# A gated delta-rule layer on one core: decay factors made ahead and read back by DMA, an earlier seed transpose, another order of PSUM banks

## The chip, the cores and the metric

One core of one Trainium2 chip runs the whole program. The metric is device time in microseconds (us), from several runs of the same kernel. One execution is profiled, and all rows below come from it.

## The reference

The input is 8 sequences of 1024 tokens, 128 features each. A layer of gated delta-rule attention (8 heads of 128, 3 Householder steps per token) is followed by a mixture of 8 experts; both have a residual and a layer norm. Cut to what matters here:

```
beta = 2 * sigmoid(x @ Wb)                        # per token, step, head
g    = -exp(A_log) * softplus(x @ Wa + dt_bias)   # per token, head
def step(S, inp):
    qt, kt, vt, bt, gt = inp
    S = S * exp(gt)
    for i in range(3):
        S = S + bt_i * outer(kt_i, vt_i - kt_i @ S)
    return S, qt @ S
```

The kernel works on chunks of 32 tokens. Inside a chunk it needs, for each pair of tokens j and t, the decay `exp(sum of g over the tokens after j, up to t)`: a table of 32 x 32 numbers per chunk and head.

## The kernel before, in words

The program has three parts: a prologue (to about 165 us of the profile) that makes per-token tables for all 256 chunks; the attention loop; and the expert part, which the change doesn't touch.

**The loop** goes over 64 superchunks of 128 tokens, four chunks (c = 0 to 3) each. Two superchunks are one turn of the hardware loop, an even one and then an odd one, so the loop's jump stands between an odd superchunk and the next even one. Each chunk has 14 slots (k = 0 to 13), written out by hand on every engine. All is float32.

- **The projection.** Slot k of chunk c projects tile m = 14c + k of the superchunk's 56 tiles on TensorE (PE) into one of three PSUM banks of `PP` (`project`, L471, matmul L478). ScalarE (ACT) makes the first convolution tap (L692), VectorE (DVE) the other three one slot later (`tap`, L780, three instructions per slot: in its slot k it works on tile k - 1), ACT the SiLU (L769). The bank of tile m is m % 3. Since 56 isn't a multiple of 3, tiles 0 and 1 meet a bank used two tiles before and not three, and `project` waits for the taps of the tile two before instead of the one three before (L476).
- **The chunk's pipeline.** Preparation of one chunk (rows of K, Gram matrices, the decayed matrices U and UQ), inversion of a triangular matrix for the one prepared before (`invert`, eight stages in the slots of `INV_AT`, L493 and L495 on PE, `inv_out` L787 and L792 on DVE), and the run of an older one (`old_state` L507, joining L610 to L624, `solve`, `read_out` L544, `new_state` L552; on DVE BZ L834 and the state S L801).
- **The seed.** GpSimd (POOL) makes the seed Y1 (L986, L988). DVE transposes it into XB in slot 13, between taps (L884, instruction L795). PE's first inversion stage in slot 1 of the next chunk (L493) multiplies by XB.
- **The decay factors.** POOL makes, for each chunk, the table GM = g times a mask (`decay`, L940). In slot 0 of chunk 0, for the four chunks of a superchunk, PE multiplies GM by the mask `after` in two matmuls of 512 columns, into PB and PK (L593, L597), and ACT takes the exponential of both into EX (L697, L699). `rows_k` and the joining matmuls of slot 2 wait for ACT there (`e_sb`). POOL multiplies EX by per-row factors into E2 (L971), from which EM comes.
- **Extras.** Chunk 2 also carries the output of an older superchunk (FA L842, WO matmuls L668); chunk 3 has the gate (L663), QSE (L825), the transposed next input in slot 12 (L469, L918).

The order of instructions on each engine is the order of the code; PE, ACT, DVE and POOL each go through their slots in turn and wait on semaphores.

Of the kernel before, what the change touches and what calls it, by code (L numbers as in the profile page):

```python
# [10 lines left out]
P = 128  # L11
# [20 lines left out]


STAGES = ["W0", "H", "H1", "H2", "W1", "H", "H1", "H2"]
assert len(STAGES) == STEPS

# [77 lines left out]
def attention_part(nc, x, Wq, Wk, Wv, Wb, Wa, A_log, dt_bias, conv_q, conv_k, conv_v, Wg, rms_weight, Wo,  # L114
                   consts, x1):
    ctx = ExitStack()
    with ctx:
# [11 lines left out]

        xf = x.rearrange("b t d -> (b t) d")  # L130


# [32 lines left out]
        with pctx:  # L165
            def psb(name, shape):
# [9 lines left out]
            Z = psb("Z", [P, NCH, NHEAD])  # L176
            Z2 = psb("Z2", [P, NCH, NHEAD])
            PXT = pctx.enter_context(nc.psum_tensor("PXT", [P, 2, 512], F32))
# [3 lines left out]
            xl_in = sems("xl_in", 2)  # L182
            xlt_ps, xlt_sb, raw_ps, raw_sb, aw_sb, bt_sb = (sem(n) for n in (
                "xlt_ps", "xlt_sb", "raw_ps", "raw_sb", "aw_sb", "bt_sb"))
# [4 lines left out]
            with nc.Block() as block:  # L189
                @block.sync  # L190
                def _(sp):
# [19 lines left out]
                    with sp.Fori(1, NLOAD // 2) as t:  # L211
                        for b in range(2):

                            sp.wait_ge(xlt_ps, 2 * t + b - 1)
                            sp.dma_start(XL[:, b], xf[bass.ds((2 * t + b) * 512, 512)].rearrange("(q p) d -> p q d", p=P)).then_inc(xl_in[b], 16)

                @block.gpsimd
                def _(pool):
                    pool.memset(WALL[:, :, :], 0.0).then_inc(wz, 1)
                    pool.memset(ones[:, :], 1.0).then_inc(wz, 1)  # L220
                    pool.memset(half4[:, :], 0.5).then_inc(wz, 1)
                    pool.memset(mhalf[:, :], -0.5).then_inc(wz, 1)

                @block.tensor
                def _(pe):
# [22 lines left out]
                    for k in range(3 * NPC, 4 * NPC):  # L248
                        pe.wait_ge(tab_sb, k - 1)
                        piece = flat(BETA)[:, PIECE * (k - 3 * NPC):PIECE * (k - 3 * NPC) + PIECE]  # L250
                        pe.matmul(PTB[:, k % 2, 0:PIECE], perm, piece, start=True, stop=True).then_inc(tab_ps, 1)

                @block.scalar
                def _(act):
# [16 lines left out]
                    for k in range(3 * NPC, 4 * NPC):  # L271
                        act.wait_ge(tab_ps, k + 1)
                        act.activation(flat(BETA)[:, PIECE * (k - 3 * NPC):PIECE * (k - 3 * NPC) + PIECE], PTB[:, k % 2, 0:PIECE], ACT.Copy).then_inc(tab_sb, 1)

                @block.vector
                def _(dve):
# [24 lines left out]
                    for s, c in enumerate((13, 11, 9, 7, 5, 3)):  # L301
# [37 lines left out]
        KDS = sb("KDS", [P, NHEAD])  # L339
        GM = sb("GM", [P, CPS, NHEAD, CT])  # L340
        EX = sb("EX", [R, CPS, NHEAD, CT])
        E2 = sb("E2", [R, NHEAD, CT])
# [38 lines left out]
        quad = PB[:, :].rearrange("p (h c) -> p h c", h=4)  # L381
        ptile = lambda m: PP[:, m % 3, 0:HALO + P]
        row_bank = lambda l, h: (PA, PK)[l][0:R, h % LH]
        lanes = [slice(0, 4), slice(4, 8)]
        heads = [range(0, 4), range(4, 8)]

        ready, begun = sem("ready"), sem("begun")
# [4 lines left out]
        gm_sb, d_ps, e_sb, kr_ps, ssr_sb, sse_sb, r2_sb, rt_sb, s1_sb, kds_sb, e2_sb, em_sb, kd_sb, kk_ps, u_sb = (  # L392
            sem(n) for n in ("gm_sb", "d_ps", "e_sb", "kr_ps", "ssr_sb", "sse_sb", "r2_sb", "rt_sb", "s1_sb", "kds_sb",
                             "e2_sb", "em_sb", "kd_sb", "kk_ps", "u_sb"))
# [42 lines left out]
        with nc.Block() as block:  # L437
            @block.sync
            def _(sp):
# [25 lines left out]
            def _(pe):  # L465
# [44 lines left out]
                def rows_k(l, i, c, sc, prep, run):  # L510
                    pe.wait_ge(kqv_sb, TILES * i - (LH if l == 0 and c == 0 else 0))
                    if l == 0 and c == 0:
                        pe.wait_ge(e_sb, 2 * i)
                    need(pe, u_sb, 2 * prep - 1 + l)
# [62 lines left out]
                def program(i, half, c):  # L577
# [7 lines left out]
                    for k in range(SLOTS):  # L585
                        if do_inv and k in INV_AT:
                            invert(invn, 1 - par, INV_AT[k])
                        if known(i, 0, NSC):
                            project(i, half, SLOTS * c + k)
                        if k == 0 and c == 0 and do_prep:  # L590
                            side_bank_free(i, c, run, do_run)
                            pe.wait_ge(gm_sb, prep + CPS)
                            pe.matmul(PB[0:R, :], after, GM[R:P, 0:2], start=True, stop=True).then_inc(d_ps, 1)  # L593
                            need(pe, s_sb, 2 * run - 1)
                            need(pe, u_sb, 2 * prep - 1)
                            need(pe, vp_sb, 2 * prep)
                            pe.matmul(PK[0:R, 0:LH], after, GM[R:P, 2:4], start=True, stop=True).then_inc(d_ps, 1)  # L597
                        if k in (1, 4) and do_run:
# [3 lines left out]
                        if k == 2 and do_run:  # L602
                            pe.wait_ge(x3t_sb, run + 1)
                            if do_prep and c == 0:
                                pe.wait_ge(e_sb, 2 * i)
# [42 lines left out]
                        if k in (8, 10) and gate_now:  # L648
                            l = (k - 8) // 2
                            if l == 0:  # L650
                                if do_run:
                                    pe.wait_ge(join_sb, 3 * run + 3)
                                else:
                                    need(pe, e_sb, 2 * i)
                                if known(i - 2, 0, NSC):
# [24 lines left out]
            def _(act):  # L680
                def program(i, half, c):
# [4 lines left out]
                    for k in range(SLOTS):  # L686
                        if known(i, 0, NSC):
# [4 lines left out]
                            act.activation(CY[:, m % RING], ptile(m)[:, 0:P], ACT.Copy, scale=taps_of(m)[:, 0:1]).then_inc(tap0_sb, 1)  # L692
                        if k == 0 and c == 0 and do_prep:
                            need(act, e2_sb, 2 * prep)
                            flat = lambda t: t.rearrange("p c h t -> p (c h t)")
                            act.wait_ge(d_ps, 2 * i - 1)
                            act.activation(flat(EX[:, 0:2]), PB[0:R, :], ACT.Exp).then_inc(e_sb, 1)  # L697
                            act.wait_ge(d_ps, 2 * i)
                            act.activation(flat(EX[:, 2:4]), PK[0:R, 0:LH].rearrange("p h c -> p (h c)"), ACT.Exp).then_inc(e_sb, 1)  # L699
                        if k in (1, 3) and do_prep:  # L700
# [74 lines left out]
            def _(dve):  # L775
# [29 lines left out]
                def group(i, half, c, k, part):  # L805
# [133 lines left out]
            def _(pool):  # L939
                def decay(ahead, i, c):  # L940
                    need(pool, d_ps, 2 * i)
                    pool.tensor_tensor(GM[R:P, c], over(G[R:P, ahead, :], [CT, NHEAD, CT], 2),
                                       over(upto[:, R:P], [CT, NHEAD, CT], 1), ALU.mult).then_inc(gm_sb, 1)
                    pool.wait_ge(gm_sb, ahead + 1)

                def program(i, half, c):
                    ahead, prep, invn, run, do_ahead, do_prep, do_inv, do_run = when(i, c)
                    par = c % 2
                    if do_run:
                        pool.wait_ge(inv_sb, STEPS * (run + 1))  # L950
                        need(pool, z_ps, 2 * run)
                        for b in range(NBK):
                            r = slice(BK * b, BK * b + BK)
                            pool.tensor_tensor(YF[r, :, r], Y3[r, :, :], over(ones[r, 0:BK], [BK, NHEAD, BK], 1), ALU.mult).then_inc(diag_sb, 1)  # L954
                            pool.wait_ge(diag_sb, NBK * run + b + 1)
                    if do_ahead:
                        decay(ahead, i, c)
                    if c == 2 and known(i - 2, 0, NSC):
# [3 lines left out]
                    if do_prep:  # L962
                        for l in range(2):
# [7 lines left out]
                            pool.tensor_tensor(E2[:, hs], EX[:, c, hs], over(S1[0:R, hs], [R, LH, CT], 2), ALU.mult).then_inc(e2_sb, 1)  # L971
                            pool.wait_ge(e2_sb, 2 * prep + l + 1)
# [449 lines left out]
```

## Time and profile before

| | us |
|---|---|
| median of 3 runs (8914.47 to 8927.09) | 8919.44 |
| profiled execution, its own time | 8925.8 |
| its span, first to last instruction | 8924.0 |
| PE busy | 7944.6 (89%) |
| DVE busy | 6744.4 (76%) |
| ACT busy | 5415.4 (61%) |
| POOL busy | 3168.8 (36%) |

The granted TensorE clock has a mean of 0.913 of the full one. A busy figure is the time in which the engine had an instruction at work; where an engine waits, a row names what ended the wait. "issue" as a releaser means that the profile shows nothing waited for; at the loop's jump it is the time until an engine has its next instructions. In a stretch's row, the column "PEclk" is the clock that was granted to TensorE.

### The profile page before, as it was taken

How to read it: one execution, taken by the hardware profiler on the slowest of the kernel's cores; microseconds unless marked ns; L12 is line 12 of the kernel's file. 1: busy time of each engine (PE TensorE's matmuls, PEld its weight loads, DVE VectorE, ACT ScalarE, POOL GpSimd, SP SyncE). 2: the span in 40 equal slices, each digit the busy share in tenths (PEclk: the TensorE clock that was granted, in tenths of full speed). 3: DMA queues.
4: the chain of work that ended last, by engine and by line, in shares of the span. 5: the costliest groups of instructions: out<-in, count | busy, mean ns of one | idle time of the engine just before them, and what ended most of it. 6: DMA issues, size and time to landing. Idle time of an engine off the chain costs nothing. (4 is left out here: it accounts for less than half of the span.)

```text
span 8924.0 us, 423618 instructions
## 1 busy us (share of the span) xinstructions
PE 7944.6 (89%) x156132; PEld 6671.9 (75%) x156132; DVE 6744.4 (76%) x22809; ACT 5415.4 (61%) x19287; POOL 3168.8 (36%) x5052
## 2 busy tenths in 40 slices
PE   3888989898889888989889898989898988979999
PEld 2677777777777777777777777777777777767777
DVE  5888888888888888888888888888888888733333
ACT  2666666666666666666666666666666666623333
POOL 0333334443433334443334343443334434411111
PEclk6899999999999999999999999999999999889999
DMA  1000000000000000000000000000000000010000
GB/s 44 4 5 6 6 6 6 6 5 6 5 6 6 6 6 6 6 5 6 6 6 6 6 5 6 5 6 6 6 6 6 6 6 5 5 28 8 9 10 8
DMA packets 72477, 64.75 MB, mean 7 GB/s; under 512 B 16944, under 2 KB 67392, under 8 KB 69952
## 3 DMA queue, kind: packets, MB, share of 16 engines
q1 hardware_dynamic: 70208, 35.32, 1.4%
q8 instruction: 1323, 21.68, 1.1%
q14 instruction: 946, 7.75, 0.3%
HBM read 26.92 MB, written 8.39 MB: 4 GB/s over the span
## 5 line engine op out<-in xcount | busy, mean ns | idle before, releaser
L780 DVE SCALAR_TENSOR_TENSOR CY<-PP,CWV,CY 128x128 f32<-128x128 f32 x4608 | 1587.9, 345 | 109.0 <-DVE CY L780 6.3
L780 DVE SCALAR_TENSOR_TENSOR CY<-PP,CWK,CY 128x128 f32<-128x128 f32 x4608 | 1585.5, 344 | 77.0
L986 POOL TENSOR_TENSOR Y<-U,C 32x256 f32<-32x256 f32 x768 | 554.5, 722 | 1223.9 <-DVE UQ L861 1183.8
L478 PE MATMUL PP<-XT,WV 128*128 128x131 f32 x3072 | 781.7, 343 | 221.6 <-issue 118.3
L692 ACT ACTIVATE CY<-PP,CWK 128x128 f32<-128x128 f32 x1536 | 562.9, 366 | 543.0 <-PE PP L478 535.0
L954 POOL TENSOR_TENSOR YF<-Y,ones 32x256 f32<-32x256 f32 x768 | 551.5, 718 | 784.0 <-DVE Y L792 743.9
L495 PE MATMUL PI<-T,WB 32*32 32x32 f32 x49152 | 722.8, 192 | 120.1 <-DVE T L792 118.9
L478 PE MATMUL PP<-XT,WK 128*128 128x131 f32 x3072 | 768.8, 338 | 68.2 <-DVE CY L780 68.2
L705 ACT ACTIVATE EM<-PK 128x128 f32<-128x128 f32 x2048 | 538.6, 280 | 474.5 <-PE PK L519 474.4
L495 PEld LDWEIGHTS PI<-T,WB 32*32 32x32 f32 x49152 | 610.5, 107 | 272.2 <-issue 202.4
L692 ACT ACTIVATE CY<-PP,CWV 128x128 f32<-128x128 f32 x1536 | 560.1, 365 | 395.5 <-PE PP L478 388.4
L493 PEld LDWEIGHTS PI<-XB,U 32*32 32x32 f32 x24576 | 353.2, 118 | 534.6 <-issue 497.7
L769 ACT ACTIVATE KQ<-CY 128x128 f32<-128x128 f32 x2048 | 740.4, 362 | 8.3
L478 PEld LDWEIGHTS PP<-XT,WV 128*128 128x128 f32 x3072 | 503.6, 208 | 315.6 <-issue 129.7
L493 PE MATMUL PI<-XB,U 32*32 32x32 f32 x24576 | 407.9, 204 | 367.8 <-DVE XB L795 367.8
L1197 ACT ACTIVATE HS<-PH,B1S 128x512 f32<-128x512 f32 x512 | 352.7, 689 | 610.0 <-PE PH L1116 610.0
L801 DVE SCALAR_TENSOR_TENSOR S<-S,WHOLE,PK 128x128 f32<-128x128 f32 x2048 | 613.4, 342 | 141.5 <-PE PK L552 141.4
L507 PE MATMUL PA<-S,KQ 128*128 128x128 f32 x4096 | 702.2, 328 | 0.0
L1125 PEld LDWEIGHTS PY<-W2S,HS 128*128 128x128 f32 x4096 | 533.9, 192 | 217.9 <-issue 214.8
L834 DVE SCALAR_TENSOR_TENSOR BZ<-PA,HEADD,VP 128x128 f32<-128x128 f32 x2048 | 618.2, 345 | 82.3 <-PE PA L507 52.8
L507 PEld LDWEIGHTS PA<-S,KQ 128*128 128x128 f32 x4096 | 656.9, 243 | 0.7 <-issue 0.2
L966 POOL TENSOR_TENSOR S<-R,BETA 96x4 f32<-96x4 f32 x512 | 101.9, 199 | 1519.3 <-DVE R L821 1519.3
(231 smaller groups left out, 19750.7 us busy)
## 6 DMA issues: line engine op xcount, KB each, us to landing
XR<-in_L_attn_x SPq DMA_DIRECT2D x65, 64.0 KB, 1.9
XL<-in_L_attn_x SPq DMA_DIRECT2D x16, 256.0 KB, 2.8
XRES<-in_L_attn_x SPq DMA_DIRECT2D x64, 64.0 KB, 1.9
x<-X SPq DMA_DIRECT2D x64, 64.0 KB, 2.0
XI<-x SPq DMA_DIRECT2D x16, 256.0 KB, 3.1
out<-OUT SPq DMA_DIRECT2D x16, 256.0 KB, 2.3
W1S<-in_L_ffn_W SPq DMA_DIRECT2D x1, 2048.0 KB
WK<-in_L_attn_Wk SPq DMA_DIRECT2D x1, 1536.0 KB, 10.2
```

The lines of the kernel that those rows point to most:

```text
L478: pe.matmul(ptile(m), w, XT[:, half], start=True, stop=True).then_inc(proj_ps, 1)
L493: mm = pe.matmul(inv[r, h], U[r, par, h, r], XB[r, h], start=True, stop=True)
L495: mm = pe.matmul(inv[r, h], WB[r, h], term[r, h], start=True, stop=True)
L507: mm = pe.matmul(PA[:, h % LH], KQ[:, rs, h, rc], S[:, h], start=True, stop=True)
L692: act.activation(CY[:, m % RING], ptile(m)[:, 0:P], ACT.Copy, scale=taps_of(m)[:, 0:1]).then_inc(tap0_sb, 1)
L705: op = act.activation(EM[:, h], PK[:, h], ACT.Square, accum_out=SSR[:, c, h:h + 1])
L769: act.activation(to, CY[:, m % RING].rearrange("p (c t) -> p c t", c=CPS), ACT.Silu).then_inc(kqv_sb, 1)
L780: dve.scalar_tensor_tensor(CY[:, m % RING], ptile(m)[:, s:s + P], taps_of(m)[:, s:s + 1], CY[:, m % RING], ALU.mult, ALU.add).then_inc(tap ...
L801: op = dve.scalar_tensor_tensor(S[:, h], S[:, h], WHOLE[:, run, h:h + 1], PK[:, h], ALU.mult, ALU.add)
L834: op = dve.scalar_tensor_tensor(BZ[:, h], PA[:, h % LH], HEADD[:, run, h:h + 1], VP[:, par, h], ALU.mult, ALU.add)
L954: pool.tensor_tensor(YF[r, :, r], Y3[r, :, :], over(ones[r, 0:BK], [BK, NHEAD, BK], 1), ALU.mult).then_inc(diag_sb, 1)
L986: pool.tensor_tensor(Y1[r, :, :], U[r, par, :, r], over(first[r, :], [BK, NHEAD, BK], 1), ALU.mult).then_inc(seed_sb, 1)
```

## The change

Before the loop, POOL makes one table of masks, SPAN; in 16 steps PE multiplies 16 chunks' g by it (two matmuls of 512 columns a step, K = 32), ACT takes the exponentials (two a step), and SP stores 128 x 1024 numbers (512 KB) to DRAM. In the loop, SP reads one chunk's factors a chunk ahead, with three DMAs, each of 256 pieces of 128 bytes, into one of two buffers. The loop's POOL instruction `decay`, its two matmuls and its two exponentials are gone, with the waits on `e_sb`, `d_ps` and `gm_sb`. DVE's transpose of the seed goes from slot 13 to slot 12, and `invert` waits for the end of the inversion before (`inv_sb`). The banks of PP follow a list, in which tiles 19 (chunk 1, slot 5) and 53 (chunk 3, slot 11) are those that meet a bank used two tiles before.

```diff
+PBANK, CLOSE = [0, 1], (19, 53)
+for _m in range(2, TILES):
+    PBANK.append(PBANK[_m - 2] if _m in CLOSE else 3 - PBANK[_m - 1] - PBANK[_m - 2])
...
+                    for w in range(NEX):
+                        sp.wait_ge(tab_sb, 4 * NPC + 2 * w + 2)
+                        sp.dma_start(exd[P * w:P * w + P], EXS[:, w % 2]).then_inc(ex_out[w % 2], 16)
+                    for b in range(2):
+                        sp.wait_ge(ex_out[b], 16 * ((NEX + 1 - b) // 2))
...
+                    pool.tensor_tensor(SPAN[R:P], over(C[R:P, C_AFTER + R:C_AFTER + P], [CT, CT, CT], 2),
+                                       over(upto[:, R:P], [CT, CT, CT], 1), ALU.mult).then_inc(span_sb, 1)
...
+                    for w in range(NEX):
+                        for f in range(2):
+                            k = 4 * NPC + 2 * w + f
+                            pe.wait_ge(tab_sb, k - 1)
+                            pe.matmul(PTB[:, f], flat(G)[R:P, P * w:P * w + P],
+                                      SPAN[R:P, CT // 2 * f:CT // 2 * f + CT // 2].rearrange("p a b -> p (a b)"), start=True, stop=True).then_inc(tab_ps, 1)
...
+                    for w in range(NEX):
+                        need(act, ex_out[w % 2], 16 * (w // 2))
+                        for f in range(2):
+                            act.wait_ge(tab_ps, 4 * NPC + 2 * w + f + 1)
+                            act.activation(EXS[:, w % 2, 512 * f:512 * f + 512], PTB[:, f], ACT.Exp).then_inc(tab_sb, 1)
...
-        ptile = lambda m: PP[:, m % 3, 0:HALO + P]
+        ptile = lambda m: PP[:, PBANK[m], 0:HALO + P]
...
+                    w = 4 * i + c - 3
+                    if known(w, 0, NCH):
+                        need(sp, e2_sb, 2 * (w - 1))
+                        rows_of = exd[bass.ds(w * NHEAD, NHEAD)] if not isinstance(w, int) else exd[w * NHEAD:(w + 1) * NHEAD]
+                        for s in range(NHH):
+                            sp.dma_start(EX[s:R:NHH, (c + 1) % 2], rows_of.rearrange("h (j t) -> j h t", j=CT)).then_inc(e_in[(c + 1) % 2], 16)
...
-                    need(pe, taps_sb, 3 * (T - 1) if m < 2 else 3 * (T - 2))
+                    need(pe, taps_sb, 3 * (T - 1) if m in CLOSE else 3 * (T - 2))
...
                     if k == 0:
+                        need(pe, inv_sb, STEPS * w)
                         pe.wait_ge(x1t_sb, w + 1)
...
-                        if k == 0 and c == 0 and do_prep:
-                            side_bank_free(i, c, run, do_run)
-                            pe.wait_ge(gm_sb, prep + CPS)
-                            pe.matmul(PB[0:R, :], after, GM[R:P, 0:2], start=True, stop=True).then_inc(d_ps, 1)
...
-                            pe.matmul(PK[0:R, 0:LH], after, GM[R:P, 2:4], start=True, stop=True).then_inc(d_ps, 1)
...
-                            if do_prep and c == 0:
-                                pe.wait_ge(e_sb, 2 * i)
-                            else:
-                                side_bank_free(i, c, run, do_run)
+                            side_bank_free(i, c, run, do_run)
...
-                            act.activation(flat(EX[:, 0:2]), PB[0:R, :], ACT.Exp).then_inc(e_sb, 1)
...
-                            act.activation(flat(EX[:, 2:4]), PK[0:R, 0:LH].rearrange("p h c -> p (h c)"), ACT.Exp).then_inc(e_sb, 1)
...
-                    if k == 13 and do_prep and part == 1:
+                    if k == 12 and do_prep and part == 1:
                         dve.wait_ge(y1_sb, prep + 1)
                         flip(XB, Y1).then_inc(x1t_sb, 1)
...
-                    if do_ahead:
-                        decay(ahead, i, c)
...
-                            pool.wait_ge(e_sb, 2 * i)
+                            pool.wait_ge(e_in[c % 2], 48 * (2 * (i - 1) + c // 2 + 1))
```

Two places of the new order are shown. First PE at the start of an even superchunk in the loop (chunk 0, slots 0 and 1), before:

```order
L478 MATMUL PP<-XT,WV 128x131
L572 ISA
L51 ISA
L593 MATMUL PB<-GM,C 96x512
L51 ISA x2
L597 MATMUL PK<-GM,C 96x512
L493 MATMUL PI<-XB,U 32x32 x24
L51 REGISTER_ALU
L478 MATMUL PP<-XT,WV 128x131
```

and now:

```order
L515 MATMUL PP<-XT,WV 128x131
L55 ISA
L520 REGISTER_ALU
L531 MATMUL PI<-XB,U 32x32 x24
L55 ISA
L515 MATMUL PP<-XT,WV 128x131
```

The two wide matmuls between the projection of tile 0 and the first inversion stage are gone; L520 is the added wait. Second, DVE in slots 12 and 13 of chunk 1 (T is the inversion's seventh stage, Y its last, X the transposed result, CY the taps), before:

```order
L792 TENSOR_TENSOR T<-Y,PI 96x256
L778 REGISTER_ALU
L51 REGISTER_ALU
L780 SCALAR_TENSOR_TENSOR CY<-PP,CWK,CY 128x128
...
L792 TENSOR_TENSOR Y<-Y,PI 96x256
L51 REGISTER_ALU
L903 STREAM_TRANSPOSE X<-Y 32x8x32 x2
...
L780 SCALAR_TENSOR_TENSOR CY<-PP,CWK,CY 128x128
L884 REGISTER_ALU
L795 STREAM_TRANSPOSE XB<-Y 96x256
```

and now:

```order
L808 TENSOR_TENSOR T<-Y,PI 96x256
...
L796 SCALAR_TENSOR_TENSOR CY<-PP,CWK,CY 128x128
L900 REGISTER_ALU
L811 STREAM_TRANSPOSE XB<-Y 96x256
L55 REGISTER_ALU
L796 SCALAR_TENSOR_TENSOR CY<-PP,CWK,CY 128x128
L800 REGISTER_ALU
L55 REGISTER_ALU x2
L808 TENSOR_TENSOR Y<-Y,PI 96x256
L55 REGISTER_ALU
L919 STREAM_TRANSPOSE X<-Y 32x8x32 x2
```

The seed's transpose now stands ahead of the last inversion stage instead of behind it.

## Rows read from the trace of the kernel before

**Rows 1.** Busy time by stretch: chunks 0 and 1 of superchunk 33; mean TensorE clock before DMA share
```profile
core 0: us, PE busy (x) PEld busy (x) DVE busy (x) ACT busy (x) POOL busy (x), PEclk, DMA share, GB/s
4044.52:4074.21 29.69, 29.34 (x576) 23.94 (x577) 21.60 (x72) 19.53 (x65) 9.28 (x17) 0.83 0.02 4
4074.21:4099.88 25.67, 22.95 (x574) 20.34 (x573) 23.52 (x78) 17.57 (x68) 11.35 (x19) 1.00 0.02 4
```

**Rows 2.** Waits, whole run: engine line tile <- who ended it: us, times, longest
```profile
DVE WB L787 <- PE PI L493: 189.1, 65, 3.6
DVE T L792 <- PE PI L495: 260.4, 293, 4.2
DVE BZ L834 <- PE PA L507: 52.8, 71, 1.8
DVE FA L842 <- ACT OGT L712: 89.2, 63, 2.2
DVE CY L780 <- issue: 48.5, 19, 2.9
PE PI L493 <- DVE XB L795: 367.8, 193, 2.1
```

**Rows 3.** Waits of DVE: chunk 0 of superchunk 33, chunk 3 of 32
```profile
DVE T L792 <- PE PI L495: 2.1, 2, 1.8
DVE T L792 <- PE PI L495: 2.0, 2, 1.7
```

**Rows 4.** Timeline of PE from chunk 3 into chunk 0: start, us, instruction, [idle before]
```profile
4044.52 0.67 PE L478 MATMUL PP<-XT,WV 128*128 128x131 f32 x2 [2.37 <-DVE CY L780]
4046.94 1.91 PE L597 MATMUL PK<-GM,C 32*96 32x512 f32 x2
4048.78 1.07 PE L493 MATMUL PI<-XB,U 32*32 32x32 f32 x48
```

**Rows 5.** Timeline of ACT, same stretch
```profile
4049.49 1.28 ACT L769 ACT_TABLE_LOAD   x1
4050.79 0.31 ACT L769 ACTIVATE KQ<-CY 128x128 f32<-128x128 f32 x1
```

**Rows 6.** Timeline at the start of chunk 2, superchunk 33: POOL, DVE, PE
```profile
4096.24 0.72 POOL L988 TENSOR_TENSOR Y<-Y,C 96x256 f32<-96x256 f32 x1
4098.20 1.11 DVE L780 SCALAR_TENSOR_TENSOR CY<-PP,CWK,CY 128x128 f32<-128x128 f32 x3
4101.90 0.69 DVE L780 SCALAR_TENSOR_TENSOR CY<-PP,CWK,CY 128x128 f32<-128x128 f32 x2
4102.12 0.70 PE L493 MATMUL PI<-XB,U 32*32 32x32 f32 x48 [1.84 <-DVE XB L795]
4102.75 0.58 PE L478 MATMUL PP<-XT,WK 128*128 128x131 f32 x1
```

**Rows 7.** Busy time by stretch: after PE's idle times, granted clock before DMA share
```profile
4044.50:4053.00 8.50, 8.48 (x69) 5.48 (x70) 4.13 (x14) 4.69 (x7) 0.71 (x2) 0.51 0.01 3
4102.10:4106.00 3.90, 3.88 (x63) 3.86 (x64) 3.76 (x14) 1.49 (x8) 0.75 (x2) 0.58 0.02 6
4076.40:4081.00 4.60, 4.55 (x146) 4.28 (x147) 4.43 (x16) 2.40 (x13) 0.87 (x2) 1.00 0.02 4
```

**Rows 8.** Timeline, chunk 3 of superchunk 31, slots 10 and 11: PE and DVE
```profile
3916.44 0.49 PE L478 MATMUL PP<-XT,WQ 128*128 128x131 f32 x2
3917.27 1.13 DVE L780 SCALAR_TENSOR_TENSOR CY<-PP,CWQ,CY 128x128 f32<-128x128 f32 x3
3918.74 0.61 DVE L801 SCALAR_TENSOR_TENSOR S<-S,WHOLE,PK 128x128 f32<-128x128 f32 x2 [0.34 <-PE PK L552]
```

**Rows 9.** Timeline of the prologue's last table matmul
```profile
151.80 0.60 ACT L273 ACTIVATE BETA<-PTB 128x512 f32<-128x512 f32 x1 [0.26 <-PE PTB L251]
```

**Rows 10.** DMA issues: size, median us from issue to landing
```profile
out<-OUT SPq DMA_DIRECT2D x16, 256.0 KB, 2.3
CWK<-in_L_attn_conv_k SPq DMA_DIRECT2D x1, 48.0 KB, 6.3
```

More of the change, by code:

```diff
@@ L31 @@
 NPC = NCH * NHEAD // PIECE
+PBANK, CLOSE = [0, 1], (19, 53)
+for _m in range(2, TILES):
+    PBANK.append(PBANK[_m - 2] if _m in CLOSE else 3 - PBANK[_m - 1] - PBANK[_m - 2])
+assert len({PBANK[-2], PBANK[-1], PBANK[0]}) == 3 and PBANK[1] not in (PBANK[-1], PBANK[0])
 STAGES = ["W0", "H", "H1", "H2", "W1", "H", "H1", "H2"]
@@ L130, in attention_part @@
         xf = x.rearrange("b t d -> (b t) d")
+        exd = nc.dram_tensor("exd", (NCH * NHEAD, CT * CT), F32, kind="Internal").ap()
         C = sb("C", [P, C_ALL])
@@ L177, in attention_part @@
             Z2 = psb("Z2", [P, NCH, NHEAD])
+            SPAN = psb("SPAN", [P, CT, CT])
+            EXS = psb("EXS", [P, 2, CT * CT])
+            NEX = NCH * NHEAD // P
             PXT = pctx.enter_context(nc.psum_tensor("PXT", [P, 2, 512], F32))
@@ L182, in attention_part @@
             xl_in = sems("xl_in", 2)
+            ex_out = sems("ex_out", 2)
+            span_sb = sem("span_sb")
             xlt_ps, xlt_sb, raw_ps, raw_sb, aw_sb, bt_sb = (sem(n) for n in (
@@ L222, in _ @@
                     pool.memset(mhalf[:, :], -0.5).then_inc(wz, 1)
+                    pool.wait_ge(w_in, 16 * NW)
+                    pool.wait_ge(wz, 4)
+                    pool.tensor_tensor(SPAN[R:P], over(C[R:P, C_AFTER + R:C_AFTER + P], [CT, CT, CT], 2),
+                                       over(upto[:, R:P], [CT, CT, CT], 1), ALU.mult).then_inc(span_sb, 1)
                 @block.tensor
@@ L251, in _ @@
                         pe.matmul(PTB[:, k % 2, 0:PIECE], perm, piece, start=True, stop=True).then_inc(tab_ps, 1)
+                    pe.wait_ge(span_sb, 1)
+                    for w in range(NEX):
[4 more added lines that the diff above has]
+                                      SPAN[R:P, CT // 2 * f:CT // 2 * f + CT // 2].rearrange("p a b -> p (a b)"), start=True, stop=True).then_inc(tab_ps, 1)
                 @block.scalar
@@ L339, in attention_part @@
         KDS = sb("KDS", [P, NHEAD])
-        GM = sb("GM", [P, CPS, NHEAD, CT])
-        EX = sb("EX", [R, CPS, NHEAD, CT])
+        EX = sb("EX", [R, 2, NHEAD, CT])
         E2 = sb("E2", [R, NHEAD, CT])
@@ L385, in attention_part @@
         heads = [range(0, 4), range(4, 8)]
+        e_in = sems("e_in")
         ready, begun = sem("ready"), sem("begun")
@@ L391, in attention_part @@
             "xt_ps", "xt_sb", "proj_ps", "tap0_sb", "taps_sb", "kqv_sb"))
-        gm_sb, d_ps, e_sb, kr_ps, ssr_sb, sse_sb, r2_sb, rt_sb, s1_sb, kds_sb, e2_sb, em_sb, kd_sb, kk_ps, u_sb = (
-            sem(n) for n in ("gm_sb", "d_ps", "e_sb", "kr_ps", "ssr_sb", "sse_sb", "r2_sb", "rt_sb", "s1_sb", "kds_sb",
+        kr_ps, ssr_sb, sse_sb, r2_sb, rt_sb, s1_sb, kds_sb, e2_sb, em_sb, kd_sb, kk_ps, u_sb = (
+            sem(n) for n in ("kr_ps", "ssr_sb", "sse_sb", "r2_sb", "rt_sb", "s1_sb", "kds_sb",
                              "e2_sb", "em_sb", "kd_sb", "kk_ps", "u_sb"))
@@ L511, in rows_k @@
                     pe.wait_ge(kqv_sb, TILES * i - (LH if l == 0 and c == 0 else 0))
-                    if l == 0 and c == 0:
-                        pe.wait_ge(e_sb, 2 * i)
                     need(pe, u_sb, 2 * prep - 1 + l)
@@ L652, in program @@
                                     pe.wait_ge(join_sb, 3 * run + 3)
-                                else:
-                                    need(pe, e_sb, 2 * i)
                                 if known(i - 2, 0, NSC):
@@ L692, in program @@
                             act.activation(CY[:, m % RING], ptile(m)[:, 0:P], ACT.Copy, scale=taps_of(m)[:, 0:1]).then_inc(tap0_sb, 1)
[L693 to L696, printed above, removed]
-                            act.activation(flat(EX[:, 0:2]), PB[0:R, :], ACT.Exp).then_inc(e_sb, 1)
-                            act.wait_ge(d_ps, 2 * i)
-                            act.activation(flat(EX[:, 2:4]), PK[0:R, 0:LH].rearrange("p h c -> p (h c)"), ACT.Exp).then_inc(e_sb, 1)
                         if k in (1, 3) and do_prep:
@@ L939, in _ @@
             def _(pool):
[L940 to L944, printed above, removed]
                 def program(i, half, c):
@@ L968, in program @@
                             pool.tensor_tensor(KDS[0:R, hs], R2[0:R, hs], TAIL[0:R, prep, hs], ALU.mult).then_inc(kds_sb, 1)
-                            pool.wait_ge(e_sb, 2 * i)
+                            pool.wait_ge(e_in[c % 2], 48 * (2 * (i - 1) + c // 2 + 1))
                             pool.wait_ge(s1_sb, 2 * prep + l + 1)
-                            pool.tensor_tensor(E2[:, hs], EX[:, c, hs], over(S1[0:R, hs], [R, LH, CT], 2), ALU.mult).then_inc(e2_sb, 1)
+                            pool.tensor_tensor(E2[:, hs], EX[:, c % 2, hs], over(S1[0:R, hs], [R, LH, CT], 2), ALU.mult).then_inc(e2_sb, 1)
                             pool.wait_ge(e2_sb, 2 * prep + l + 1)
```

4 lines of the change are left out of this document (removed).

## The prediction

> **What bounds the kernel now.** I read the busy times first, then busy time by stretch, then who waited for whom, then the timeline at the places with the longest waits. PE and DVE do nearly all the limiting: no engine is busy all the time, since the slots hand work to and fro between the two. The attention loop is what the change can move.
>
> The four chunks of a superchunk have nearly the same work, and chunk 1 has no extras, so it shows what a chunk costs when nothing stands in its way: 25.67 us, at full clock [rows 1]. Chunk 0 has no extra but the decay matmuls, and takes 29.69 us, with a granted clock of 0.83 [rows 1]. The reader should see that DVE works less in chunk 0's stretch (21.60 us) than in chunk 1's (23.52 us): chunk 0 is long because DVE waits. So I count the time by DVE's waits. The whole-run list gives them [rows 2]: WB, the first inversion result, 189.1 us in 65 waits; T, a later stage, 260.4 us; BZ 52.8 us; FA 89.2 us. One superchunk in each pair of them also has 2.9 us at the loop's jump ("issue") [rows 2]; that stays.
>
> Where does WB's wait come from? At the boundary PE stands still for 2.37 us until DVE has done the taps of tile 54 (the rule for tile 0), restarts at 4044.52, runs the two wide decay matmuls, and only at 4048.78 the first inversion stage [rows 4]. DVE has meanwhile run dry. PE also pays with its clock: from 4044.5 to 4053 it was granted 0.51 of full speed, the lower level of 1.2 GHz, after those 2.37 us of idling [rows 7]. The same stage in chunks 1 to 3 waits for the transposed seed, 367.8 us in 193 waits, 1.9 us each [rows 2]. After one of these, 1.84 us long [rows 6], the clock fell (0.58), after another of 1.8 us it stayed at 1.00 [rows 7]. That wait is PE's and costs DVE nothing by itself; it costs by starting PE late, and by the clock.
>
> **The change, part by part.** There are 62 full superchunks (31 odd, 31 even).
>
> *Decay matmuls and exponentials out of the loop.* PE goes from the projection of tile 0 straight to the inversion stage, whose operands are there, while DVE is still in slot 0. WB's wait goes: 189 us. BZ's wait, for a PE at half clock, goes: 53 us. T's waits in chunk 0 were 2.1 us in an odd superchunk [rows 3]; with PE not idling for 2.4 us there, they go in the odd ones: 31 x 2.1 = 65 us. In the even ones the jump idles PE anyway and its clock stays low, so I leave theirs in. Sum: 307 us. What is late next is DVE itself, as in chunk 1. POOL's `decay` costs nothing, since POOL is the engine with the most idle time, and its removal gives nothing. On ACT each superchunk loses two exponentials and two table loads. A load takes 1.28 us, and the next activation starts at 4050.79, 0.02 us after the load's end [rows 5]. The Trainium skill ("ScalarE: Activation LUTs", section "What ACT_TABLE_LOAD costs") charges a switch of table with a drain of some 1.4 us besides; by that each of the two would give 1.4 us more, up to 170 us if all of it lay on the path. The row shows no such drain, so I take none.
>
> *The seed's transpose in slot 12.* Its work on DVE is moved, not added. POOL finishes the seed of chunk 1 at 4096.96, and DVE's slot 12 runs its taps from 4098.20 [rows 6], so it should not wait. The first inversion stage can then follow the projection of tile 0 as soon as the inversion before is done, and what holds PE is the next projection, for the taps of slot 13. These ended at 4102.59 and would end 0.43 us (the transpose) sooner, at 4102.16; the projection started at 4102.75 [rows 6], so PE is 0.6 us earlier in slots 1 to 3. Bounds for what DVE gains: with the clock falling as before, 0.6 us in chunk 3 (its T wait) and 0.55 in chunk 2 (FA), together 71 us. With the clock staying up, all of FA's wait (89), 1.75 us of the 2.0 of T's in chunk 3 [rows 3] (109) and the small rest in chunk 1 (18): 216 us. Below nothing is excluded unless DVE waits for the seed. The idle time is cut from about 1.85 us to 1.2, and of two such waits of the old length one kept the clock, so I take the middle, 144 us.
>
> *The other bank order.* Tile 19 waits for tile 17's taps. PE meets that point just as they end (chunk 1, slot 5, where PE has nothing but the projection), so it costs nothing. Tile 53 is another matter. Its projection started at 3916.44, in slot 11 of chunk 3; it will have to wait for the taps of tile 51, which are the first two instructions of the group that starts at 3917.27, some 0.74 us of its 1.13 [rows 8]. That is 3918.0, or 1.6 us later. Behind it on PE stand `read_out` and `new_state`, for which DVE's S at 3918.74 already waited (0.34 us) [rows 8], and after them the transposed input of slot 12. PE and DVE are level there, so I charge all of it: 62 x 1.6 = 99 us. Below, the cost would be nothing if S were late anyway. The old rule for tiles 0 and 1 is gone with the 2.37 us that are counted above.
>
> *The prologue.* It ends with one matmul of 512 columns per 0.60 + 0.26 = 0.86 us [rows 9]. The new 32 take 28 us if PE sets the pace. A store of 512 KB isn't in the trace; one of 256 KB lands in 2.3 us [rows 10]. With 2.7 to 4.6 us for the double and two buffers, a step takes 2.0 to 2.9 us (half of two exponentials and a landing), 16 steps 32 to 47 us, plus the last landing of 3, less the 4 us that DVE worked on alone at the end. That is 31 to 46 us; I take 38.
>
> *The loads.* 768 pieces of 128 bytes per chunk, requested when the chunk before has been used, so with a chunk's time, 25.67 us, to land. The nearest row for small pieces is CWK, 3072 pieces of 16 bytes in 6.3 us [rows 10]; three such in a row are 18.9 us, a small one about 2. Either fits, so they cost nothing. SP has only issues to do and little queued.
>
> **Sum**: 307 + 144 - 99 - 38 = 314 us off the profiled execution's 8925.8: 8612. The median is 6 us below that execution, so **8605 us**.
>
> **The rivals.**
>
> - *The clock stays up everywhere.* For it: shorter idle times of PE in all chunks. Against: the jump, and the new wait in slot 11. 307 + 216 - 99 - 38 = 386: 8534 us.
> - *The clock falls as before.* For it: it fell after 1.84 us [rows 6, 7], and 1.2 us isn't far. Then BZ and T keep their waits: 189 + 71 - 99 - 46 = 115: 8805 us.
> - *Slower: the new wait in slot 11 of chunk 3.* PE idles 1.6 us there and the clock may fall before some 6 us of dense PE work that DVE awaits. At half clock (8.5 us at 0.51 elsewhere [rows 7]) that is about 4 us per superchunk, 248 us. On top of the case before: 115 - 248 = -133, 9052 us. It decides from 115/62 = 1.9 us per superchunk on. Against it: the stretch just before it is dense.
> - *Slower: loads land late.* Each us beyond the chunk's 25.67 costs 250 us, so 30 us would give about 9700. The row of 16-byte pieces speaks against it. The Trainium skill ("DMA: Bandwidth & Descriptors", section "Specifications") says that pieces under 512 bytes are below line rate and cost a read-modify-write; these have 128. By that rule this is the case to fear.
>
> **How the numbers follow.** Forecast 0.45, clock up 0.22, clock down 0.20, slot 11 0.06, late loads 0.03, and 0.04 for gains that cancel near nothing. A measurement of this kernel can tell 0.2% (18 us) from no change. Faster: 0.45 + 0.22 + 0.20 and a little of the last, 0.88; within 0.2%: 0.03; slower: 0.09. The range takes in the clock-up case with a cheap prologue and half of slot 11's charge unpaid (8534 - 7 - 50, about 8480) and the clock-down case (to 8810).
>
> **What the profile should show.** WB's wait near nothing, and chunk 0 of an odd superchunk about as long as chunk 1. No table loads in the loop. The wait of the first inversion stage for XB gone, its place taken by a shorter one for taps or for Y. A new wait of PE in slot 11 of chunk 3, with a longer one of DVE's S. A prologue longer by 31 to 46 us, and E2 never waiting for a DMA. The forecast is wrong if DVE's waits turn up elsewhere in the same slots, if POOL's seed is late for slot 12, or if the clock's mean, now 0.913, doesn't rise.

## The result, and the profile after

The changed kernel takes 8546.44 us (median of 4 runs, 8534.73 to 8553.03), the kernel before 8916.95 us beside it; the ratio is 0.9582, with a 95% interval of 0.9566 to 0.9599. That is 373 us off 8919. The forecast was 8605 us, so the sign, the range and most of the size are right. The profiled execution, 12 us under the median, has a span of 8532.9 us, 391 less than before. Its page:

```profile
span 8532.9 us, 423951 instructions
PE 7574.3 (89%) x155940; PEld 6385.2 (75%) x155940; DVE 6721.0 (79%) x22809; ACT 5198.6 (61%) x19063; POOL 3013.5 (35%) x4797
...
q1 hardware_dynamic: 281408, 68.93, 3.7%
...
EX<-exd SPq DMA_DIRECT2D x768, 32.0 KB, 2.2
exd<-EXS SPq DMA_DIRECT2D x16, 512.0 KB, 2.6
```

The page shows the change as made: 768 new loads with a median of 2.2 us to landing, 16 stores, and DMA queues still almost empty. TensorE's mean granted clock went from 0.913 to 0.957.

The waits of the whole run answer to [rows 2]. The columns are us in total, times, longest; the list's other lines are left out:

```profile
PE PP L515 <- DVE CY L796: 544.0, 546, 3.3
DVE S L817 <- PE PK L588: 259.0, 257, 8.8
DVE T L808 <- PE PI L533: 42.5, 112, 2.1
DVE XT L934 <- PE PB L506: 35.0, 64, 2.2
DVE BZ L850 <- PE PA L545: 3.2, 3, 1.3
DVE WB L803 <- PE PI L531: 2.2, 2, 1.9
DVE FA L858 <- ACT OGT L728: 1.8, 1, 1.8
```

Against before, DVE's wait for WB fell by 187 us, for T by 218, for FA by 87 and for BZ by 50: 542 us. S's wait rose from 141.4 to 259.0, by 118, and XT's from 11.0 to 35.0, by 24. The prologue is 48 us longer: the first projection starts at 214.35, before at 166.64. 542 - 118 - 24 - 48 is 352 of the 391 us. Of the remaining 39, DVE's busy time fell by 23; the other 16 I don't place. PE no longer waits for XB at all; the first line shows what holds it now, the taps.

The stretches of superchunk 33, chunks 0 to 3, answer to [rows 1]:

```profile
3876.10:3901.10 25.00, 23.28 (x574) 20.27 (x573) 23.22 (x78) 17.15 (x66) 10.59 (x18) 1.00 0.05 10
3901.10:3926.61 25.51, 23.17 (x575) 20.25 (x573) 23.48 (x78) 17.53 (x68) 10.73 (x18) 1.00 0.04 7
3926.61:3956.03 29.42, 25.97 (x598) 22.88 (x596) 25.89 (x93) 21.63 (x89) 12.96 (x20) 1.00 0.04 7
3956.03:3988.90 32.87, 26.73 (x605) 22.62 (x606) 27.40 (x91) 19.49 (x73) 12.87 (x21) 0.94 0.05 11
```

Chunk 0 was 29.69 us at a clock of 0.83 and is now 25.00 at 1.00. The same boundary as in [rows 4] on PE:

```profile
3876.10 0.39 PE L515 MATMUL PP<-XT,WV 128*128 128x131 f32 x2
3876.42 0.70 PE L531 MATMUL PI<-XB,U 32*32 32x32 f32 x48
3877.98 0.49 PE L515 MATMUL PP<-XT,WV 128*128 128x131 f32 x2 [0.87 <-DVE CY L796]
3878.31 1.05 PE L545 MATMUL PA<-S,KQ 128*128 128x128 f32 x8
```

The inversion stage follows the projection of tile 0 at once and takes 0.70 us, where it took 1.07 at half clock [rows 4]; the idle time of 2.37 us ahead of tile 0 is gone, and one of 0.87 stands ahead of tile 1. Chunk 3 shows the new wait (superchunk 45, slots 10 to 12, answering to [rows 8]):

```profile
5326.28 1.07 PE L686 MATMUL PB<-WG,XT 128*32 128x256 f32 x16
5328.90 0.49 PE L515 MATMUL PP<-XT,WQ 128*128 128x131 f32 x2 [1.55 <-DVE CY L796]
5329.32 0.65 PE L580 MATMUL PA<-BZ,UQ 128*32 128x128 f32 x16
5329.90 1.89 PE L588 MATMUL PK<-BZ,KD 96*128 96x128 f32 x8
```

`new_state` takes 1.89 us here, where it took 1.16 at full clock before: in this superchunk the clock fell after the wait. The stretches from 5325.86 show it (same columns as [rows 1]):

```profile
5325.86:5328.90 3.04, 1.49 (x25) 0.71 (x19) 2.74 (x9) 1.43 (x5) 2.57 (x4) 1.00 0.00 0
5328.90:5332.72 3.82, 3.82 (x74) 3.21 (x75) 1.12 (x5) 0.95 (x3) 0.00 (x0) 0.66 0.00 0
5332.72:5337.14 4.42, 4.42 (x70) 4.01 (x64) 2.24 (x10) 1.38 (x5) 0.00 (x0) 0.52 0.02 4
```

Slots 11 and 12 took 8.2 us there. Over superchunks 1 to 63 PE's idle time ahead of slot 11 is 1.55 us nearly everywhere, but the clock fell in these two slots in 15 of them: 12 took 8.2 to 8.3 us, 3 took 6.8, and the other 48 took 5.2. So the rival of slot 11 did occur, in about one superchunk of four.

### The profile page after: what moved, and what is told of

Same layout as the page of the kernel before. It is cut to its first block and busy times, and to the rows that moved or that the text cites. A ratio compares the mean times of both kernels' runs of the same rounds, so it can differ in the third digit from the quotient of the medians.

```text
span 8532.9 us, 423951 instructions
## 1 busy us (share of the span) xinstructions
PE 7574.3 (89%) x155940; PEld 6385.2 (75%) x155940; DVE 6721.0 (79%) x22809; ACT 5198.6 (61%) x19063; POOL 3013.5 (35%) x4797
## 5 line engine op out<-in xcount | busy, mean ns | idle before, releaser
L515 PE MATMUL PP<-XT,WV 128*128 128x131 f32 x3072 | 758.6, 334 | 247.2 <-DVE CY L796 209.3
L515 PE MATMUL PP<-XT,WK 128*128 128x131 f32 x3072 | 743.0, 328 | 242.7 <-DVE CY L796 232.3
L817 DVE SCALAR_TENSOR_TENSOR S<-S,WHOLE,PK 128x128 f32<-128x128 f32 x2048 | 612.5, 341 | 259.2 <-PE PK L588 259.0
L515 PEld LDWEIGHTS PP<-XT,WV 128*128 128x128 f32 x3072 | 476.7, 197 | 373.8 <-DVE CY L796 296.5
L515 PEld LDWEIGHTS PP<-XT,WK 128*128 128x128 f32 x3072 | 468.3, 194 | 362.1 <-DVE CY L796 322.4
L796 DVE SCALAR_TENSOR_TENSOR CY<-PP,CWQ,CY 128x128 f32<-128x128 f32 x1536 | 528.4, 344 | 114.8 <-ACT CY L715 64.0
L545 PE MATMUL PA<-S,KQ 128*128 128x128 f32 x4096 | 600.9, 295 | 1.2 <-DVE BZ L850 1.2
L588 PE MATMUL PK<-BZ,KD 96*128 96x128 f32 x4096 | 589.2, 289 | 0.0
```

Of the source, the lines that this page charges most:

```text
L545: mm = pe.matmul(PA[:, h % LH], KQ[:, rs, h, rc], S[:, h], start=True, stop=True)
L588: mm = pe.matmul(PK[:, h], KD[:, rc, h], BZ[0:R, h], start=True, stop=True)
L796: dve.scalar_tensor_tensor(CY[:, m % RING], ptile(m)[:, s:s + P], taps_of(m)[:, s:s + 1], CY[:, m % RING], ALU.mult, ALU.add).then_inc(tap ...
L817: op = dve.scalar_tensor_tensor(S[:, h], S[:, h], WHOLE[:, run, h:h + 1], PK[:, h], ALU.mult, ALU.add)
```

## The experiments

All times are ratios to the kernel before on the same chip, with their interval; "on 8919" turns a ratio into us with the median of the kernel before. The whole change is 0.9582, -373 us on 8919.

### Which part brings what

**Tiles 19 and 47.** Edit to the changed kernel:

```diff
-PBANK, CLOSE = [0, 1], (19, 53)
+PBANK, CLOSE = [0, 1], (19, 47)
```

> The changed kernel with tiles 19 and 47 (chunk 3, slot 5) instead of 19 and 53 as those that meet a bank used two tiles before. Theory (the wait of slot 11 is on the path): PE has only a projection in slot 5 and stands 0.2 us behind the taps there, so the wait is free; S's wait falls back from 259 to about 141 us, XT's from 35 to about 10, and the clock no longer falls in slots 11 and 12 of some chunks 3. 100 to 140 us less than the changed kernel: 8405 to 8446 us. Rival (DVE is bound by something else in chunk 3, the wait only took the place of another): within 20 us of 8546.

Measured: 8409.43 us, ratio 0.9447 (0.9435 to 0.946), -493 us on 8919. It is 120 us under the changed kernel. Its waits:

```profile
DVE S L817 <- PE PK L588: 141.9, 255, 6.1
...
DVE T L808 <- PE PI L533: 48.1, 117, 4.0
```

S's wait is back at 142 us, and that alone is 117 us. The wait in slot 11 was on the path, as the forecast had it. With it went the low clock: in slots 11 and 12 it fell in none of the 63 superchunks. The close tile in slot 5 shows in DVE's list by little (T's wait is 6 us longer, U's 5).

**Old banks.** The changed kernel with `m % 3` and tiles 0 and 1:

```diff
-        ptile = lambda m: PP[:, PBANK[m], 0:HALO + P]
+        ptile = lambda m: PP[:, m % 3, 0:HALO + P]
...
-                    need(pe, taps_sb, 3 * (T - 1) if m in CLOSE else 3 * (T - 2))
+                    need(pe, taps_sb, 3 * (T - 1) if m < 2 else 3 * (T - 2))
```

> The changed kernel with the banks of the kernel before (m % 3, the two close tiles are 0 and 1). Theory: the wait of slot 11 goes (about 117 us of S's wait), but PE is held before tile 0 until DVE's slot 13 is done and before tile 1 until slot 0 is done, behind which stand the first inversion stage, old_state and rows_k; that costs about 1 to 2 us per superchunk in WB, BZ and T waits and lets the clock fall again at the boundary. 8480 to 8600 us. Rival (decay out of the loop makes these waits harmless): 8420 us, as with tiles 19 and 47.

Measured: 8570.1 us, ratio 0.9624 (0.9611 to 0.9637). The old rule costs 38 us more than slot 11's wait. DVE's wait for T is back in part, that for BZ in full (52.8 before):

```profile
DVE S L817 <- PE PK L588: 143.2, 256, 8.4
DVE T L808 <- PE PI L533: 141.4, 195, 2.2
...
DVE BZ L850 <- PE PA L545: 65.0, 67, 1.3
```

So a good bank order is worth 158 us once the rest is in place (0.9624 against 0.9447), and the chosen one gives back 120 of them.

**Seed in slot 13.** The changed kernel with the transpose where it was:

```diff
-                    if k == 12 and do_prep and part == 1:
+                    if k == 13 and do_prep and part == 1:
```

> The changed kernel with the seed's transpose back in slot 13. Theory: PE waits for XB again in all four chunks, 1.8 to 1.9 us each, starts slots 1 to 3 later and loses its clock in some of them: FA's and T's waits come back, 71 to 216 us more than 8546: 8617 to 8762 us. Rival (the transpose's place is neutral once the decay matmuls are gone): 8546 within 20 us.

Measured: 8791.47 us, ratio 0.9874 (0.9859 to 0.9889), so 260 us more than the changed kernel, beyond the upper end that I gave. The mean clock fell to 0.922.

```profile
PE PI L531 <- DVE XB L811: 426.8, 224, 2.2
```

The wait for XB comes 224 times now, before 193: chunk 0 has it too, but nearly only in the odd superchunks (32 times, twice in even ones), not behind the loop's jump. T's wait is 110 us longer than in the changed kernel, FA's 69 and S's 34; the clock fell in slots 11 and 12 of 31 superchunks, not 15.

**Seed in slot 12 alone.** The kernel before with this one move and its wait:

```diff
+                        need(pe, inv_sb, STEPS * w)
                         pe.wait_ge(x1t_sb, w + 1)
...
-                    if k == 13 and do_prep and part == 1:
+                    if k == 12 and do_prep and part == 1:
```

> The kernel before with the seed's transpose in slot 12 and the added wait, nothing else. Theory: chunks 1 to 3 gain what the forecast gave to this part, 71 to 216 us, chunk 0 little, since the decay matmuls stand ahead of its first inversion stage: 8700 to 8846 us. If the clock is what counts, the mean granted clock rises from 0.913 to over 0.93 and the time is at the lower end. Rival (early start alone, clock as before): 8846.

Measured: 8663.22 us, ratio 0.9737 (0.9724 to 0.9751), -235 us on 8919; the clock's mean rose to 0.943. One instruction moved by one slot, with the wait that it needs, is worth more than all the rest of the change as made.

**Banks alone.** The kernel before with the new list of banks (the PBANK lines of the change, tiles 19 and 53).

> The kernel before with the new bank order alone (tiles 19 and 53). Theory: the 2.4 us of PE before tile 0 become shorter (the projection no longer waits for tile 54), but the seed is still transposed at the end of slot 13 and the decay matmuls can only move up by some 2 us, while slot 11 costs 1.9 us per superchunk (S's wait rises by about 118 us, as with the whole change). Within 80 us of 8902, more likely faster than slower. Rival (the bank order is worth something only with the other two): slower by 60 to 120 us.

Measured: 8910.86 us, ratio 0.9982 (0.9969 to 0.9995), -16 us: what the boundary gains, slot 11 takes back.

```profile
DVE S L805 <- PE PK L556: 278.1, 257, 10.4
...
DVE WB L791 <- PE PI L497: 78.8, 31, 3.0
```

WB's wait fell by 110 us, S's rose by 137. By superchunk the list shows something that the forecast missed: what is left of WB's waits stands in the even superchunks (78 of the 79 us), behind the loop's jump. In the odd ones the bank order alone takes WB's wait away, with the wide decay matmuls still in place, and T's waits in their chunk 0 fall from 63 to 17 us. In the even ones T's stay at 49.

**Decay alone.** The changed kernel with the seed in slot 13 and the old banks (the edits of both experiments above).

> Decay factors from DRAM alone: seed in slot 13, old banks. The forecast gave this part 307 less 38 us. With seed and banks in place it measured as about 8663 - 8570 = 93 us only, so WB's wait is not the decay matmuls' alone. Theory: the first inversion stage waits for the transposed seed at the end of slot 13 and PE is at half clock after that; the decay matmuls filled this time partly. 93 to 150 us faster than 8902: 8750 to 8810 us. Rival (the forecast): 8633 us.

Measured: 8781.79 us, ratio 0.9837 (0.9825 to 0.985), -145 us on 8919. WB's wait is gone, but T, FA (96.8 us) and BZ stay, and PE waits for XB:

```profile
DVE T L808 <- PE PI L533: 237.1, 277, 2.2
...
DVE BZ L850 <- PE PA L545: 66.6, 71, 1.4
...
PE PI L531 <- DVE XB L811: 366.9, 192, 2.2
PE PP L515 <- DVE CY L796: 339.9, 323, 3.3
```

In chunk 0 by itself T's waits are 121 us, before 112: the decay part alone takes nothing off them, nor off BZ's (52.8 before). With the bank order beside it (the run with the seed in slot 13) they are 28 and 6 us.

**Seed and tiles 19 and 47, decay in the loop.** The kernel before with both edits.

> The kernel before with the seed in slot 12 and the banks with tiles 19 and 47; the decay factors still made in the loop. It tells what the decay part is worth in the best surroundings. If the parts add up as measured (seed alone 0.9737, banks free of slot 11's wait some 0.012 more): ratio 0.958 to 0.966, 8545 to 8616 us, so that the decay part brings another 120 to 190 us to 8430. Rival (PE is so far ahead with seed and banks that the decay matmuls hide): within 60 us of tiles 19 and 47 with the whole change.

Measured: 8584.53 us, ratio 0.9627 (0.961 to 0.9644), within what was expected of parts that add up. The decay part is thus worth another 0.018 (about 160 us) in the best surroundings.

The corners tried, on 8919: seed 235, decay 145, banks 16; seed and decay 335; decay and banks 112; all three 373; all three with tiles 19 and 47 493. Seed and decay add up to 380 and bring 335 together. The banks with tile 53 bring 16 alone, cost 33 beside the decay part and bring 38 beside both; with tile 47 they bring 98 beside the seed and 158 beside both. With tile 47 alone or beside the decay part alone they weren't run.

### Is it the clock or the early start?

**Idle time filled.** The kernel before, with matmuls that nobody reads ahead of the first inversion stage in chunks 1 to 3:

```diff
                         if do_inv and k in INV_AT:
+                            if k == 1 and c > 0 and known(i, 0, NSC):
+                                need(pe, inv_sb, STEPS * invn)
+                                for z in range(7):
+                                    pe.matmul(PI[:, 256:384], ident, WQ[:, 0], start=True, stop=True)
                             invert(invn, 1 - par, INV_AT[k])
```

> The kernel before, with seven matmuls of 128 columns (some 1.5 us, read by nobody) on PE in front of the first inversion stage of chunks 1 to 3, in the idle time in which it waits for the transposed seed. The work of the inversion starts no earlier. Theory (the clock is a large part of what the early seed is worth): the mean granted clock rises from 0.913 to over 0.94, FA's and T's waits in chunks 2 and 3 shrink, and the time falls by 60 to 130 us against 8919. Rival (the early start is all of it): within 20 us of the kernel before, or slower by what the filling outlasts the wait.

Measured: 8750.15 us, ratio 0.9806 (0.9792 to 0.9819), -173 us on 8919, for some 1300 added matmuls (7 in each of 186 chunks) and nothing taken away. The start of chunk 2 of superchunk 33, as PE's timeline and as granted clock (the last row is the start of its chunk 3):

```profile
4014.78 1.72 PE L590 MATMUL PI<-WQ,C 128*128 128x128 f32 x14
4016.79 0.70 PE L493 MATMUL PI<-XB,U 32*32 32x32 f32 x48 [0.28 <-DVE XB L799]
```

```profile
4017.40:4021.00 3.60, 3.60 (x104) 3.37 (x96) 3.49 (x13) 2.58 (x17) 0.33 (x1) 1.00 0.02 7
...
4047.66:4052.00 4.34, 4.34 (x110) 4.06 (x102) 4.27 (x17) 2.81 (x13) 0.30 (x1) 1.00 0.08 19
```

The inversion stage waits for XB as before, only 0.28 us of the idle time are left, and the clock is 1.00 where it was 0.58 [rows 7]. FA's wait fell from 89.2 to 35.1 us, T's from 260.4 to 135.2:

```profile
DVE T L796 <- PE PI L495: 135.2, 202, 4.2
...
DVE FA L846 <- ACT OGT L716: 35.1, 63, 2.2
```

The clock is thus most of what the early seed brings (173 of 235 us, if the two compare); the early start is the rest.

### What of the decay part counts?

**Exponentials back.** The changed kernel, ACT, slot 0 of chunk 0:

```diff
+                        if k == 0 and c == 0 and do_prep:
+                            for z in range(2):
+                                act.activation(EXD[:, z], HEADD[0:R, 0:64, :].rearrange("p a b -> p (a b)"), ACT.Exp)
```

> The changed kernel with two exponentials on ACT in slot 0 of chunk 0, of a table in SBUF into a tile that nobody reads; they bring the two table loads back. Theory (ACT isn't what is waited for): less than 30 us slower than 8546, since 3.8 us of ACT's time per superchunk fit into its idle time, but taps of tile 1 and the squares of chunk 0 come later, up to 62 x 1.5 = 90 us. Rival (ACT was on the path in the kernel before): 62 x 3.8 = 235 us slower.

Measured: 8715.3 us, ratio 0.9762 (0.9749 to 0.9775), 160 us more than the changed kernel. Neither of my two figures fits; the cost is far above the 30 to 90 us of the theory. ACT's timeline and PE's at one boundary:

```profile
3970.56 1.28 ACT L719 ACT_TABLE_LOAD   x1
3971.85 1.15 ACT L719 ACTIVATE EXD<-HEADD 96x512 f32<-96x512 f32 x2
3973.01 1.28 ACT L789 ACT_TABLE_LOAD   x1
3974.31 0.31 ACT L789 ACTIVATE KQ<-CY 128x128 f32<-128x128 f32 x1
...
3977.38 0.31 ACT L789 ACTIVATE KQ<-CY 128x128 f32<-128x128 f32 x1
```

```profile
3977.75 0.65 PE L556 MATMUL PK<-C,KQ 128*128 128x128 f32 x4 [1.76 <-ACT KQ L789]
```

ACT spends 3.7 us on the table loads and exponentials, works on without a pause, and does the last SiLU of the superchunk's Q tiles only at 3977.38. `rows_k` in slot 3 waits for it, so PE idles for 1.76 us, and in the stretch from 3977.7 to 3984 the granted clock is 0.64. Over the whole run PE's waits of `rows_k` for KQ rise from 26 to 88 us, and the mean clock falls from 0.957 to 0.937.

**Copies in their place.** The same with `ACT.Copy` for `ACT.Exp`, so without table loads:

> As exps_back, with two copies on ACT in the place of the two exponentials, so without table loads. Theory (ACT's time in slot 0 counts nearly one to one, 3.8 us cost 2.7 us a superchunk): 1.2 us of copies cost 0.2 to 0.9 us a superchunk, 12 to 55 us over the changed kernel. Rival (any instruction there costs as much, through the order of ACT): near the 160 us of exps_back.

Measured: 8536.18 us, ratio 0.9574 (0.9559 to 0.9589), no different from the changed kernel. So 1.2 us of work on ACT are free there, and the 2.57 us that the two table loads add are what costs; that they do so by their length alone, since they pass the point at which `rows_k` waits, is argued from the timeline. What was put back costs 160 us beside tile 53, and the decay part with tiles 19 and 47 is worth 208 us before paying 48 for the prologue. If the two compare, the table loads carry most of it; no run took them alone out of the kernel before, and the two wide matmuls weren't tried by themselves.

**Loads four times.** Three more loads for each, into a tile that nobody reads, and POOL waits for all twelve:

```diff
+                            for z in range(3):
+                                sp.dma_start(EXJ[s:R:NHH, 3 * ((c + 1) % 2) + z], rows_of.rearrange("h (j t) -> j h t", j=CT)).then_inc(e_in[(c + 1) % 2], 16)
...
-                            pool.wait_ge(e_in[c % 2], 48 * (2 * (i - 1) + c // 2 + 1))
+                            pool.wait_ge(e_in[c % 2], 192 * (2 * (i - 1) + c // 2 + 1))
```

> The changed kernel with every load of decay factors issued four times (three of them into a tile that nobody reads), and POOL waiting for all of them: 12 DMAs and 3072 pieces of 128 bytes per chunk. Theory (the loads are hidden by a whole chunk): 8546 within 20 us; 12 landings of 2.2 us one behind the other would take 26 us, so they must overlap for this to hold. Rival (small pieces disturb others or land late): slower by more than 50 us, with waits of E on a DMA.

Measured: 8538.26 us, ratio 0.957 (0.9558 to 0.9583), no difference, and POOL's list has no wait for them. Four times the small pieces still land within a chunk.

### The prologue

**Four store buffers**, with tiles 19 and 47:

```diff
-            EXS = psb("EXS", [P, 2, CT * CT])
+            EXS = psb("EXS", [P, 4, CT * CT])
...
-                            act.activation(EXS[:, w % 2, 512 * f:512 * f + 512], PTB[:, f], ACT.Exp).then_inc(tab_sb, 1)
+                            act.activation(EXS[:, w % 4, 512 * f:512 * f + 512], PTB[:, f], ACT.Exp).then_inc(tab_sb, 1)
...
```

> The changed kernel with tiles 19 and 47 and four buffers instead of two for the prologue's stores. Theory (the prologue's new steps are slow because PE waits for the first stores and drops to half clock, 1.65 us per matmul where 0.86 is possible): the first tile's projection starts at about 195 us and not at 214, 10 to 25 us less than tiles 19 and 47 alone: ratio about 0.943. Rival (the stores themselves set the pace, about 2.6 to 3.3 us per step): no difference.

Measured: 8404.62 us, ratio 0.9422 (0.9409 to 0.9435). The lowest time of all, but the interval meets that of two buffers (0.9435 to 0.946), and the first projection starts at 215.27 against 216.25. Both my readings failed; the rival's time came true, but not for its reason. The stores don't set the pace: PE is busy all the time and at half clock. First with two buffers (the changed kernel), then with four:

```profile
158.00:200.00 42.00, 42.00 (x50) 15.03 (x49) 0.00 (x0) 14.93 (x25) 0.00 (x0) 0.50 0.39 154
```

```profile
146.00:157.00 11.00, 11.00 (x21) 3.94 (x22) 3.48 (x2) 5.81 (x10) 0.00 (x0) 0.81 0.15 59
159.00:200.00 41.00, 41.00 (x49) 14.99 (x49) 0.00 (x0) 14.31 (x25) 0.00 (x0) 0.50 0.38 154
```

In the second kernel PE wasn't idle ahead of the fall either, so the first stores don't cause it. At 0.50 a 512-column matmul takes about 1.7 us, and 32 of them, the first few faster, some 50. This was readable before: the first table matmuls of the old prologue were as slow (last section).

## Where the prediction was right, and where it was not

- **Chunk 0 becomes like chunk 1**: right, 25.00 us against 25.51. WB (187 us) and BZ (50) went as charged (189 and 53).
- **T's waits in chunk 0 of even superchunks** I left in, "the jump idles PE anyway and its clock stays low". They went too: T's wait is 42.5 us in all. In chunk 0 of the even ones they fell from 49 to 7 us, so the step "31 x 2.1 = 65" left out 42. It was also put to the wrong part: with the decay part alone T's waits in chunk 0 (121 us, before 112) and BZ's stay.
- **The seed, 144 us**: mis-sized. It measured 235 alone and 260 on top of the other two. I took the middle between "clock falls" and "clock stays"; the waits of the seed alone show the upper end (FA 89.2 to 1.8, T 260.4 to 126.3). That its value is mostly the clock was the mechanism of the upper bound, and the filled idle time shows it.
- **The decay part, 307 us less 38**: the waits counted under it vanished, but it didn't bring them all. Alone it gives 145 us, 193 with the prologue's 48 added back. The 307 held the end of the old rule for tiles 0 and 1 as well ("counted above"), and that was needed: in odd superchunks the bank order alone takes WB's wait and most of T's in chunk 0 away, and in even ones T's and BZ's go only with both. WB's wait was the end of one chain (PE idle for the taps, half clock, wide matmuls, table loads), and I credited the whole chain to one link. Both links together, without slot 11, come to an estimated 112 + 48 + 120 = 280 us, near the 307.
- **The sum was closer than its parts**, and that is luck. Against 307 + 144 - 99 - 38 = 314 stand 280 + 260 - 120 - 48 = 372. The seed's term was 116 us too small, twice the distance from 8605 to 8546; the other three errors (27, 21 and 10) go the other way and took half of it back.
- **ACT off the path**: wrong. I took "none" for the table loads beyond their place in WB's wait. They cost 160 us where they are put back into the changed kernel, 2.6 us per superchunk, through the order of ACT and one wait of `rows_k`. The Trainium skill's drain behind each switch ("ScalarE: Activation LUTs", "What ACT_TABLE_LOAD costs") again has no row here: the activation at 3974.31 follows the load, 3973.01 + 1.28, within 0.02 us. But the section's weight on switches of table was the right hint for this change, and my weighing of its drain passed over the loads themselves.
- **The bank order, 99 us**: mechanism and place right, size 120 (S's wait 118, XT's 24). PE's wait was 1.55 us, as charged. What the 15 superchunks lose in which the clock falls after it (3 us each in 12, 1.5 in 3, together some 41) is more than the excess of 21; it was the slower rival's mechanism, at a small part of its price.
- **The prologue, 38 us**: 48 measured, by another cause than either of mine. I took 0.86 us per matmul from the last row of the old prologue, at a high clock; the 32 ran at 0.50.
- **The loads**: right, free even fourfold. The rule on pieces under 512 bytes (the Trainium skill, "DMA: Bandwidth & Descriptors", "Specifications") changes no time here: 32 KB in 256 pieces land in 2.2 us.
- **Clock stays up**, the rival at 8534 us, came nearest in its sum; the forecast stood between it and the clock-down case. Its condition did not hold: the clock still fell in slots 11 and 12 of 15 superchunks.

## What to carry to other kernels

Where two engines hand work to and fro, look for the instruction that the waiting engine's restart hangs on and ask whether it can stand earlier among work that needs nobody: one transpose moved ahead of a group of taps, an inversion stage and two other transposes was worth 2.6%. Price an idle time of TensorE at its length plus what a trace shows at half clock after it, which here was not after each; filling it with matmuls that nobody reads is a cheap test of that. Credit a wait at the end of a chain to a link only after undoing that link alone.

## What the runs showed of the hardware that I had not expected

Matmuls on 32 rows of 512 columns ran for 42 us with PE busy without a pause at a granted clock of 0.50, in both kernels with the new prologue; in the kernel before the same holds for its first 20 us of table matmuls, and the clock rose only among the 128-row ones that follow:

```profile
126.00:146.00 20.00, 20.00 (x24) 6.55 (x22) 1.12 (x2) 6.56 (x11) 0.00 (x0) 0.50 0.00 0
148.20:152.00 3.80, 3.56 (x6) 1.10 (x5) 0.00 (x0) 2.00 (x4) 0.00 (x0) 0.75 0.00 0
```

In the changed kernel the clock was still high (0.85 over 146 to 155) in the first of the new matmuls and fell among them. No run here varied the rows, so a cause isn't shown. Second, PE's idle times of the same length had different ends: after 1.55 us ahead of slot 11 of chunk 3 the clock fell in 15 superchunks and stayed in 48.
